# Keys' and queries' products in pairs on column halves, and the inverse's 64-level on four row groups

## The reference

```
pred  = k_t . S
delta = (v_t - pred) * beta_t
S     = S + k_t (outer) delta
o_t   = q_t . S
```

## Time and profile before

| | us |
|---|---|
| median of 3 runs | 538.74 |
| the runs | 532.18, 542.06, 538.74 |
| span of the profiled execution, first to last instruction | 539.8 |
| TensorE busy in that span | 489.4 (91%) |
| VectorE, ScalarE, GpSimd busy | 330.4, 325.2, 325.4 |
| mean granted TensorE clock | 0.955 |

### The profile page before, as it was taken

One profiled execution on the slowest core, in us unless ns is written; L12 is line 12 of the kernel. 1 busy time (PEld: TensorE's weight loads), 2 busy tenths in 40 slices (PEclk: granted clock), 3 DMA queues, 4 the chain that ended last, 5 costly groups with the idle time before them and its releaser, 6 DMA issues.

```text
span 539.8 us, 18897 instructions
## 1 busy us (share of the span) xinstructions
PE 489.4 (91%) x7053; PEld 403.7 (75%) x7053; DVE 330.4 (61%) x1321; ACT 325.2 (60%) x905; POOL 325.4 (60%) x445
## 2 busy tenths in 40 slices
PE   6979989999999999999997887999999999999910
PEld 4666767767777777676765577999999999999910
DVE  4436558758778686776876762556445565455445
ACT  2645767777768877677664632555555555555454
POOL 3053717867678676786764542376667776767662
PEclk9998999999999999999988878999999999999965
DMA  3358664672554735547183223254536545453367
GB/s 93 31 85 224 215 149 46 94 106 26 73 47 57 101 35 72 49 58 95 24 174 36 32 31 103 36 109 56 109 56 127 110 57 107 60 123 35 30 129 213
DMA packets 154804, 46.09 MB, mean 85 GB/s; under 512 B 107168, under 2 KB 149280, under 8 KB 154720
## 3 DMA queue, kind: packets, MB, share of 16 engines
q1 hardware_dynamic: 132848, 29.86, 28.5%
q0 software_dynamic: 20288, 9.51, 18.9%
q10 hardware_dynamic: 1584, 5.59, 2.7%
HBM read 21.39 MB, written 23.55 MB: 83 GB/s over the span
## 4 chain that ended last, share of the span: by engine, by line
PE 73%; DMA 7%; DVE 7%; issue 6%; ACT 2%; SPq 2%; POOL 1%; ACTq 0%; DVEq 0%; POOLq 0%
PE ps L986 16%; PE ps L997 10%; PE ps L724 5%; PE ps L709 4%; PE ps L681 3%; PE ps L768 2%; PE ps L684 2%; PE ps L758 2%; PE ps L876 2%; PE ps L748 2%; PE ps L850 2%; PE ps L1012 2%; PE ps L780 2%; PE ps L738 2%; PE ps L685 2%
## 5 line engine op out<-in xcount | busy, mean ns | idle before, releaser
L1771 POOL DMA_INDIRECT x_store<-xk,row x80 | 125.1, 1563 | 68.8 <-ACT xk L1258 49.3
L1730 POOL DMA_INDIRECT slots_in<-x,slot x64 | 99.4, 1553 | 29.3 <-issue 17.8
L1589 DVE TENSOR_TENSOR hb<-ps,hs 128x320 f32<-128x320 f32 (+1 forms) x128 | 62.6, 492 | 51.0 <-ACT hs L1250 47.4
L1250 ACT ACTIVATE hs<-ps 128x320 f32<-128x320 f32 (+1 forms) x128 | 55.4, 435 | 34.5 <-PE ps L986 28.9
L986 PE MATMUL ps<-xeTh,w13h 128*128 128x320 f32 x224 | 71.2, 318 | 1.4 <-DVE xeTl L1613 1.0
L986 PE MATMUL ps<-xeTl,w13h 128*128 128x320 f32 x224 | 69.8, 312 | 0.0
L986 PE MATMUL ps<-xeTh,w13l 128*128 128x320 f32 x224 | 69.8, 311 | 0.0
L997 PE MATMUL ps<-w2s,hb 128*128 128x128 f32 x512 | 64.8, 279 | 1.0 <-DVE hb L1589 0.6
L997 PEld LDWEIGHTS ps<-w2s,hb 128*128 128x128 f32 x512 | 59.9, 192 | 3.5 <-DVE hb L1589 1.5
L1712 POOL TENSOR_TENSOR prod<-a,xs 128x28 f32<-128x28 f32 (+11 forms) x120 | 32.7, 272 | 31.5 <-DVE xs L1422 22.8
L1258 ACT ACTIVATE xk<-ps,gs 128x128 f32<-128x128 f32 x80 | 24.2, 365 | 44.5 <-PE ps L1012 34.9
(11 more groups left out here) (210 smaller groups left out, 1109.3 us busy)
## 6 DMA issues: line engine op xcount, KB each, us to landing
slots_in<-zeros ACTq DMA_DIRECT2D x10, 520.0 KB, 5.3
xe<-slots_in SPq DMA_DIRECT2D x15, 325.0 KB
w<-w_in SPq DMA_DIRECT2D x8, 448.0 KB
xTs<-xT SPq DMA_DIRECT2D x4, 512.0 KB, 4.9
a_diag<-hb SPq DMA_DIRECT2D x64, 32.0 KB
inv<-xs SPq DMA_DIRECT2D x16, 128.0 KB
xi<-inv SPq DMA_DIRECT2D x16, 128.0 KB
xk<-x SPq DMA_DIRECT2D x8, 256.0 KB, 5.2
```

The lines of the kernel that those rows point to most:

```text
L1250: af(hs[to, s % 4, :], ps[src, HB[fill_of(s) % 5], 0:HALF], ACT.Silu).then_inc(hs_ready, 1)
L1589: v.tensor_tensor(hb[to, par, c, HALF * g:HALF * g + HALF], ps[rows_, at, 0:HALF], hs[rows_, s % 4, :], ALU.mult).then_inc(h_ready, 1)
L1730: g.indirect_dma_start(out=xs_d[:, :], out_offset=bass.IndirectOffsetOnAxis(ap=to, axis=0), in_=x1[:, p % 2, j, k, :], in_offset=None, com ...
L1771: g.indirect_dma_start(out=x1_d[:, :], in_=ye[:, par, i, :], in_offset=None, out_offset=bass.IndirectOffsetOnAxis(ap=row[:, par, i:i + 1], ...
```

## The change

It edits four things.

1. `key_key` and `key_query` of a turn become `key_pair(n, m, b)`, which makes the product of keys of chunk n and that of keys and queries of chunk m, both of sequence b, as four matmuls of 64 output rows: rows 64 to 127 of the first and rows 0 to 63 of the second with all 512 columns, then the other rows with only the 256 columns that are read.
2. In `z_64` and `w_64` the units of the second sequence take the transposed form, so that their matmuls use the row groups that those of the first leave free. The results of `w_64` for the second sequence go to bank OB, so `w_64` now waits for `orms_out`. The sign moves from `t64_copy` into `z64_copy`, which is one instruction on 128 partitions instead of two on 32; `x64_turned` is two instructions instead of eight.
3. The halves of bank LV swap their roles for the levels of 64 and 128.
4. The orders of the fills and of the lists of TensorE, ScalarE and VectorE are new.

```diff
-LV, ZA, CB, OB, MB = 3, 4, 5, 6, 7
+LV, OB, ZA, CB, MB = 3, 4, 5, 6, 7
-STEP_FILLS = (("v", 1, 0), ("kk", 1, 0), ("kq", 5, 1), ("g", 4, 0), ("gq", 4, 0), ("gq", 4, 1), ("kk", 1, 1),
-              ("y", 0, 0), ("kq", 4, 0), ("y", 0, 1))
+STEP_FILLS = (("kk", 1, 0), ("kq", 5, 0), ("gq", 4, 0), ("g", 4, 0), ("kk", 1, 1), ("kq", 5, 1), ("gq", 4, 1),
+              ("y", 0, 0), ("y", 0, 1), ("v", 0, 0))
...
+            def key_pair(n, m, b):
+                kk, kq = 0 <= n < NP, 0 <= m < NP
+                if kk:
+                    pe.wait_ge(y_free, 2 * n + 2)
+                    to_k = free_bank("kk", n, b)
...
+                if kq:
+                    pe.wait_ge(gq_out, 2 * m + 2)
+                    to_q = free_bank("kq", m, b)
...
+                apart(pe)
+                if kk:
+                    mm(ps[64:128, to_k, :], kT[:, 64:128], ys.rearrange("p h t -> p (h t)"), start=True, stop=True)
+                if kq:
+                    mm(ps[0:64, to_q, :], qT[:, 0:64], gs_.rearrange("p h t -> p (h t)"), start=True, stop=True)
+                if kk:
+                    mm(ps[0:64, to_k, :].rearrange("p (h t) -> p h t", h=H)[:, :, 0:64], kT[:, 0:64], ys[:, :, 0:64],
+                       start=True, stop=True).then_inc(fill_mm, 1)
+                if kq:
+                    mm(ps[64:128, to_q, :].rearrange("p (h t) -> p h t", h=H)[:, :, 64:128], qT[:, 64:128],
+                       gs_[:, :, 64:128], start=True, stop=True).then_inc(fill_mm, 1)
...
@@ z_64
-                for u in range(U):
+                for h in range(H):
                     for m in range(2):
                         s, t = slice(64 * m, 64 * m + 32), slice(64 * m + 32, 64 * m + 64)
-                        last = mm(ps[s, LV, 32 * u:32 * u + 32], A[t, n % AR, u, s], x32T[t, n % 2, u, :],
+                        mm(ps[s, LV, 256 + 32 * h:288 + 32 * h], A[t, n % AR, h, s], x32T[t, n % 2, h, :],
+                           start=True, stop=True)
+                        last = mm(ps[t, LV, 256 + 32 * h:288 + 32 * h], A[s, n % AR, H + h, t], x32[s, H + h, :],
                                   start=True, stop=True)
@@ w_64
                 pe.wait_ge(z64_out, n + 1)
+                if n:
+                    pe.wait_ge(orms_out, n)
...
-                        last = mm(ps[s, LV, 256 + 32 * u:256 + 32 * u + 32], x32[s, u, :], z64[s, u, :],
+                        mm(ps[s, LV, 32 * h:32 * h + 32], x32[s, h, :], z64[s, h, :], start=True, stop=True)
+                        last = mm(ps[s, OB, 32 * h:32 * h + 32], z64[t, h, :], x32T[t, n % 2, H + h, :],
                                   start=True, stop=True)
@@ TensorE's list
-                at(values, p - 1)
                 at(turn_keys, p - 5)
-                at(key_key, p - 1, 0)
+                at(project, p - 6)
                 at(z_128, p - 5)
-                at(project, p - 6)
...
-                at(key_query, p - 5, 1)
+                key_pair(p - 1, p - 5, 0)
                 at(w_128, p - 5)
+                at(queries, p - 4, 0)
                 at(gate_in, p - 4)
-                at(queries, p - 4, 0)
                 at(deltas, p - 5)
+                key_pair(p - 1, p - 5, 1)
                 at(state_queries, p - 5)
+                at(turn_deltas, p - 5)
                 at(queries, p - 4, 1)
-                at(turn_deltas, p - 5)
-                at(key_key, p - 1, 1)
...
                 at(new_state, p - 5)
-                at(key_query, p - 4, 0)
+                at(head_sums, p - 5)
+                at(keys, p, 1)
                 at(z_64, p - 4)
                 at(state_keys, p - 4)
-                at(head_sums, p - 5)
-                at(keys, p, 1)
+                at(values, p)
                 at(w_64, p - 4)
@@ ScalarE's list
+                at(z128_copy, p - 7)
                 at(key_key_out, p - 3, 0)
-                at(z128_copy, p - 7)
                 at(t128_copy, p - 7)
-                at(x1_rstd, p - 8)
                 at(queries_out, p - 6, 0)
                 at(deltas_out, p - 7)
                 at(gate_out, p - 6)
+                at(x1_rstd, p - 8)
+                at(key_key_out, p - 3, 1)
                 at(deltas_turned, p - 7)
-                at(key_key_out, p - 3, 1)
...
-                at(softmax, p - 8)
-                at(gate_sigmoid, p - 6)
-                at(key_norms, p - 5)
                 clear(p, 0)
                 at(queries_out, p - 6, 1)
+                at(softmax, p - 8)
...
                 at(outputs_out, p - 7)
-                at(t_diag, p - 6)
+                at(gate_sigmoid, p - 6)
+                at(key_norms, p - 5)
...
-                at(keys_out, p - 2, 0)
                 at(head_norms, p - 7)
...
+                at(t_diag, p - 6)
                 clear(p, 3)
+                at(keys_out, p - 2, 0)
                 at(keys_out, p - 2, 1)
                 at(x64_diag, p - 6)
@@ VectorE: z64_copy, t64_copy, x64_turned
-                for m in range(2):
-                    s = slice(64 * m, 64 * m + 32)
-                    last = v.tensor_copy(z64[s], ps[s, LV, 0:256].rearrange("p (u c) -> p u c", u=U))
-                last.then_inc(z64_out, 1)
+                v.tensor_scalar(z64[:], ps[:, LV, 256:384].rearrange("p (h c) -> p h c", h=H), -1.0, None,
+                                ALU.mult).then_inc(z64_out, 1)
...
-                    last = v.tensor_scalar(TT[s, :, 64 * m + 32:64 * m + 64],
-                                           ps[s, LV, 256:512].rearrange("p (u c) -> p u c", u=U), -1.0, None, ALU.mult)
+                    last = v.tensor_copy(
+                        TT[s, :, 64 * m + 32:64 * m + 64].rearrange("p (b h) c -> p b h c", b=B),
+                        ps[s, LV:OB + 1, 0:128].rearrange("p b (h c) -> p b h c", h=H))
...
-                for u in range(U):
-                    b, h = u // H, u % H
-                    last = v.transpose(x64[64 * b + 32:64 * b + 64, h, 0:32], TT[0:32, u, 32:64])
+                for b in range(B):
+                    last = v.transpose(x64[64 * b + 32:64 * b + 64, :, 0:32], TT[0:32, H * b:H * b + H, 32:64])
@@ VectorE's list
-                at(masked, p - 5, 0)
                 at(z64_copy, p - 5)
                 at(keys_read, p - 5)
                 at(gated_values, p - 6)
-                at(t64_copy, p - 5)
                 at(gated_out, p - 6)
+                at(t64_copy, p - 5)
                 at(x64_turned, p - 5)
                 at(residues, p - 5)
...
+                at(masked, p - 5, 0)
                 at(normalise, p - 6)
-                at(masked, p - 5, 1)
                 at(experts, p - 6)
                 at(inverse_in, p - 4)
+                at(masked, p - 5, 1)
                 at(offsets, p - 6)
```

More of the change, by code:

```diff
@@ L257, in build @@
         x32 = sb("x32", [P, U, 32])
-        z64 = sb("z64", [P, U, 32])
+        z64 = sb("z64", [P, H, 32])
         x64 = sb("x64", [P, H, 64])
@@ L704, in values @@
                 last.then_inc(fill_mm, 1)
-            def key_key(n, b):
-                pe.wait_ge(y_free, 2 * n + 2)
-                to = free_bank("kk", n, b)
-                mm(ps[:, to, :], xTs[:, b, cols(n)], y[:, n % YR, b].rearrange("p h t -> p (h t)"),
-                   start=True, stop=True).then_inc(fill_mm, 1)
             def queries(n, g):
@@ L719, in queries @@
                 last.then_inc(fill_mm, 1)
-            def key_query(n, b):
-                pe.wait_ge(gq_out, 2 * n + 2)
-                to = free_bank("kq", n, b)
-                mm(ps[:, to, :], xTs[:, b, cols(n)], gq[:, n % 2, b].rearrange("p h t -> p (h t)"),
-                   start=True, stop=True).then_inc(fill_mm, 1)
+            def key_pair(n, m, b):
[3 more added lines that the diff above has]
+                    to_k = free_bank("kk", n, b)
+                    kT = xTs[:, b, cols(n)]
+                    ys = y[:, n % YR, b]
+                if kq:
+                    pe.wait_ge(gq_out, 2 * m + 2)
+                    to_q = free_bank("kq", m, b)
+                    qT = xTs[:, b, cols(m)]
+                    gs_ = gq[:, m % 2, b]
+                apart(pe)
[9 more added lines that the diff above has]
+                       gs_[:, :, 64:128], start=True, stop=True).then_inc(fill_mm, 1)
             def gate_in(n):
@@ L763, in w_64 @@
                 pe.wait_ge(z64_out, n + 1)
+                if n:
+                    pe.wait_ge(orms_out, n)
+                else:
+                    pe.wait_ge(setup_dve, 4)
                 apart(pe)
-                for u in range(U):
+                for h in range(H):
                     for m in range(2):
-                        s = slice(64 * m, 64 * m + 32)
-                        last = mm(ps[s, LV, 256 + 32 * u:256 + 32 * u + 32], x32[s, u, :], z64[s, u, :],
+                        s, t = slice(64 * m, 64 * m + 32), slice(64 * m + 32, 64 * m + 64)
+                        mm(ps[s, LV, 32 * h:32 * h + 32], x32[s, h, :], z64[s, h, :], start=True, stop=True)
```

(9 more changed lines are left out.)

## The result

| | before | after |
|---|---|---|
| median, us (12 runs each) | 534.29 | 537.11 |
| lowest and highest | 531.37 to 542.06 | 533.86 to 541.12 |
| ratio, with its 95% interval | | 1.008 [1.0048, 1.0112] |
| the same two on another chip | 537.27 | 537.10, ratio 0.9977 [0.9931, 1.0022] |

The account below looks back on a forecast made before the run. TensorE's order was taken to bound turns 5 to 16: 15.41 + 0.6 + 0.25 = 16.26 us against 17.15, 10.7 us in 12 turns, plus 1.5 elsewhere; 538.74 - 12 gives 527 us, own range 522 to 532, overall 519 to 538.

Parts of the forecast that it names:

- The base: Whole kernel before: median 538.74 us, from which 12 us were subtracted; the profiled execution's span was 539.8.
- The products: Key and query products on TensorE: two pairs of column halves 2.89 us against 3.73, minus 0.84 a turn in 12 turns.
- The 64-level: z_64 and w_64 on TensorE: four matmuls at once, 0.37 us instead of 0.62, minus 0.25 each in 16 turns.
- Work in all: TensorE's work per turn: 16.75 - 0.84 - 0.50 = 15.41 us.
- What is moved: Groups in new places, such as project between w_64 and z_128: cover there 1.25 us instead of 2.35.
- The first new wait: Between w_64 and z_128: z_128 waits 0.6 us a turn (bounds 0.3 and 0.9) for a 1.85 us chain.
- The second wait: ScalarE between head_sums and w_128, now with more work there: 0.25 us a turn (bounds 0 and 0.7).
- I cost it at nothing: Inverse's DMA loads for the solve: inverse_in keeps about two microseconds in hand, so no cost.
- The rival of the clock: Waits before z_128 drop TensorE's clock in each of 16 turns, 1.55 us each: 552 us, chance 0.05.

Follow-up runs that it names:

- the one-pair kernel: Kernel before with the new 64-level, one pair of products on column halves and project ahead of z_128, other two products whole: 532.60 us, ratio 0.9943 to before.
- the first kernel with earlier norms: Changed kernel with ScalarE's gate_sigmoid and key_norms moved back ahead of queries_out(1) and outputs_out: 541.43 us, median of 6, no ratio.

## Why the prediction was wrong

**The base.** The median of 3 runs, 538.74, from which I subtracted, lay 4.4 us above the median of 12. And the execution profiled before, with a span of 539.8, was a long one, 9.5 us above the second profile. Its steady turns were ordinary. Its tail was not: from `turn_deltas` of turn 16 to that of turn 20 it took 66.6 us, the second profile 307.10 - 246.61 = 60.5; and after turn 20, where the change touches nothing, it took 228.0 against 223.2. Between 245 and 330 us the clock stood at half at 255, 272, 289 and 306 in the first, and in the second only near 257. Measured against the second profile (span 530.3, 1.8 below the change's), the change is ahead by 246.61 - 242.17 = 4.4 us at turn 16 and behind by 308.43 - 307.10 = 1.3 at turn 20, a tail longer by 5.8 us. Its own second profile loses 3.9 there, and against the first profile of before neither loses anything. Two profiles of each don't settle it: on average the tail is 63.6 us before and 65.4 after, and the steady turn 17.11 and 16.94.

**The products: right.** Halves run side by side; a pair is 1.44 us against 1.39, all products came 0.92 lower against 0.84 forecast.

**The 64-level: right,** 0.24 each against 0.25. `z_64` writes from four row groups into one bank, each to its own 32 partitions, and its 32 records start some 0.01 us apart. By the rule of the Trainium skill, TensorEngine Tiling (Array Packing), section Restrictions and Gotchas, that different row tiles cannot access the same PSUM bank simultaneously, `z_64` would have kept its 0.62 us; the trace doesn't agree, with 0.39.

**"Work in all" failed, by 0.6 us a turn.** I took 1.34 us off and 0.77 came off, because I priced the neighbours of a group only at the pairs (0.10 behind each, and 0.11 once more). In the new order `turn_keys`, `deltas`, `values` and `project` have neighbours of another tiling, and these four take 0.61 us more. The kernel with the order alone isolates it: 0.67 us more work a turn and 0.79 with the waits, without any of the savings. "What is moved" was costed for its covers, not for its neighbours. The Trainium skill, TensorEngine Tiling (Array Packing), section Key Properties, says that changing the tiling mode drains TensorE; it gives no price, the rows show 0.14 us more on `turn_keys` (0.35 against 0.21) and 0.18 a turn on `deltas`. That tiling is the cause of all 0.61 is not shown: no run changed a tiling alone, and two rows speak against so simple a rule. `turn_keys` got another tiling only ahead of it, where `values` had stood before without taking more. And `head_sums` takes 0.50 us instead of 0.35 in the kernel with the old order and the new 64-level, between two groups of its own tiling. In twelve turns 0.57 us is 6.8 of the 12 us forecast.

**The first new wait was right in mechanism and nearly in size.** `z_128` started 2.0 to 2.2 us after `w_64` in every turn of the first profile, since `gated_out` and `t64_copy` have to be done first. I took 1.85 us for that chain, and 0.6 for the wait; waits grew by 0.34 in the first profile and by 0.70 in the second. In one turn out of two it is the longer, 0.55 instead of 0.20 (at 185.90 and at 202.25), because a copy starts late beside a scatter. That was to be seen before too, had I looked at VectorE and GpSimd in another turn of before:

```profile
221.19 0.85 DVE L1380 TENSOR_SCALAR TT<-ps 32x256 f32<-32x256 f32 x2 [1.88 <-PE ps L768]
```

```profile
219.95 1.55 POOL L1730 DMA_INDIRECT slots_in<-x,slot  x1 [0.30 <-issue]
```

`w_64` began at 219.29 and its records ended at 219.98, but `t64_copy` started 1.2 us later, as long after the scatter's start. **The second wait**, `w_128` for `z128_copy`, did not come: in the turn shown `w_128` starts 0.31 us after the pair's last record did, with no wait.

**"I cost it at nothing": failed, in the tail.** I wrote that the inverse's round trip through DRAM kept its two microseconds in hand, and named `z_32` waiting for `inverse_in` as what would prove it wrong. In steady turns nothing waits for it. In turn 18 of before it had 2.6 us in hand by the first profile and 0.1 by the second, so that the two microseconds were not there to spend. Turns 17 and 18 became 2.6 us faster each (1.9 against the second profile). The smaller work doesn't explain it: the kernel with the order alone, with all the work of before, takes 29.0 us for the two, the change 28.1, and the kernels of the old order with their scatters 32.0 to 35.7, with the savings or without (28.8 without scatters). Here the new order is quicker, and I had taken 0.3 us a turn for everything. GpSimd did not become faster. Its two turns (eight scatters, a solve of 12 us, `silu` and `Vk`) take 33.3 us with some 4.1 of waiting, so 29.2 of its own, and TensorE's turns 17 and 18 together take 28.1. So in the profile of the change GpSimd came along as the chain, 24% of it against 1% (8% in the second). Then the wait of 2.26 us took about half of what the two turns had saved, and the slow clock behind it the rest. Without scatters both vanish in the change, at turns of 14 us. They don't in the kernel of before without scatters (a wait of 2.70 us, a turn 19 of 18.0) nor in the one-pair kernel (2.42 and 19.1), whose solves start with their input. So two things lie close together in the tail, GpSimd's queue and the round trip through DRAM itself, and taking away the first uncovers the second.

**The rival of the clock** had the right price and the wrong place. I set it in front of `z_128` in each turn, where the clock row keeps its highest digit from the fifth slice on until half of the span is over; waits of 0.55 us didn't bring it down. In the loop of the first profile it fell once, behind the wait of 2.26 us, and it stayed down for 17.1 us, where I had taken 3 from the earlier trace rows. Turn 19 of the two kernels with unused products is 2.2 and 2.5 us shorter, about half a per cent; their ratios, 1.0022 against 1.008 and 0.9857 against 0.9943, come from different chips. They agree in direction, but 1.0022 lies above the 0.9977 of the change's second measurement.

**What stays open.** Whether the change costs 0.8% or nothing: two chips gave 1.008 [1.0048, 1.0112] and 0.9977 [0.9931, 1.0022], and where ten runs or more of a kernel were made on one chip, they differ by 7 to 19 us. Single turns of 18 us and more, in some runs and not in others, make part of it; in one of them (turn 9 of the first kernel with earlier norms) TensorE ran dry inside the records of `w_32` for 0.6 and 0.5 us with nothing to be seen that it waited for, and I have not tried to find the cause.

## What to carry to other kernels

When an order is rewritten so that a cheaper instruction fits, price each neighbour: groups that got a neighbour of another tiling were longer by 0.1 to 0.2 us here, and a few of those ate almost half of a saving of 1.3. Test the order with the old work in it first; that one run (17.94 against 17.15 us a turn) would have said what the change could bring. Where a stage ends and the engine that bounded it gets less to do, look for the loop on the quiet engine that comes next, and for the one behind that, and profile before more than once, since a tail of 66.6 us in one execution was 60.5 in the next.

## What the runs showed of the hardware

**Many operations released during an indirect DMA of GpSimd start late.** In turns 8 to 16 of the first profile of the change, TensorE releases 28 copies on VectorE and ScalarE during a scatter (1.55 us). Of these 17 start 1.29 to 1.51 us after the scatter began, which is 0.23 to 1.03 us after their release (1.2 us in the row of before above). The other 11 start 0.03 to 0.08 us after it, as nearly all do outside of a scatter, and nearly all of the kernel without scatters. Operations already following one another on VectorE, such as L1409, L1460 and L1465 at 183.35 to 184.14, run on within a scatter. The Trainium skill, SBUF — State Buffer, section SBUF: two separate sides, says that VectorE and GpSimd share a port pair that one of them holds exclusively. This doesn't look like it: `t64_copy` reads PSUM and is late, `osl` reads two operands in SBUF and isn't. The late ones of the first profile were always the same (`z64_copy`, `t64_copy`, and `deltas_out` and `t128_copy` on ScalarE); in the second there are others too, up to 1.5 us late. What picks them is open.

**A fall of TensorE's clock can last a whole turn.** After 2.26 us without work in the tail it was at 0.50 for 17.1 us, though PE was busy for 16.30 of them, while after 0.97 us in the earlier trace rows it was 3.5 us. The length of the wait didn't decide it: behind 2.62 us it was 10.4 us (second profile of the change), behind 2.42 us 6.9 (one pair), and behind 2.70 us 3.5 (before without scatters). Twelve unused products of 2.92 us in the gap kept the clock up there in both kernels that had them; in the first of these it fell 5 us later, behind a wait of 1.28 us, for 6.9 us.
